# Places and load times of the contexts of a single-head attention, order of early loads, and who makes the first normalized chunks, in a four-layer transformer kernel

## The reference, cut to what matters

```python
# L0: keys and values from the normalized, modulated context
xkv = _ada_ln(x_kv, t_vec, Wss_kv, bss_kv)      # (x-mean)/sqrt(var+eps) * (1+scale) + shift
kv  = (xkv @ Wkv + bkv).reshape(B, Lkv, 2, nh, dh)
attn = softmax(einsum('bqhd,bkhd->bhqk', q, k) / sqrt(dh));  x = x + (attn @ v) @ Wp + bp
# L1: one head; the raw context is the prototype bank
nx = _layer_norm(x, ln_gamma, ln_beta);  q = nx @ Wq
k = prototype_bank @ Wk;  v = prototype_bank @ Wv
weights = softmax(einsum('bth,bph->btp', q, k) * H ** -0.5)
evidence = einsum('btp,bph->bth', weights, v)   # then a router, three experts and a gate
```

## Time and profile before

| | us |
|---|---|
| median of 3 runs (lowest, highest) | 958.58 (958.03, 962.11) |
| the profiled execution | 953.42 |
| its span, first to last instruction | 951.6 |
| TensorE busy in it | 839.7 (88%) |
| VectorE busy | 607.5 (64%) |
| ScalarE busy | 500.2 (53%) |
| GpSimd busy | 366.8 (39%) |
| chain of work that ended last: TensorE, VectorE, GpSimd, DMA | 61%, 16%, 6%, 3% |

### The profile page before, as it was taken

One profiled execution on the slowest core, in us unless ns is written; L12 is line 12 of the kernel. 1 busy time (PEld: TensorE's weight loads), 2 busy tenths in 40 slices (PEclk: granted clock), 3 DMA queues, 4 the chain that ended last, 5 costly groups with the idle time before them and its releaser, 6 DMA issues.

```text
span 951.6 us, 22830 instructions
## 1 busy us (share of the span) xinstructions
PE 839.7 (88%) x9532; PEld 543.2 (57%) x9532; DVE 607.5 (64%) x1274; ACT 500.2 (53%) x753; POOL 366.8 (39%) x482
## 2 busy tenths in 40 slices
PE   6689999998997897877999999888786799999986
PEld 4256677765655344534777776544452466666653
DVE  6877787776231663736777777535374677777825
ACT  7367777775232205234777776522413467767541
POOL 8666666630000034165666662010313333333000
PEclk9799999999899998878999999999788799999999
DMA  9954444357145106253444433010417244443100
GB/s 263 242 142 131 132 131 132 99 174 229 66 141 164 53 1 175 65 146 92 130 131 124 134 93 93 2 66 11 132 46 179 74 131 131 134 138 107 49 2 10
DMA packets 76838, 106.89 MB, mean 112 GB/s; under 512 B 9370, under 2 KB 70426, under 8 KB 76480
## 3 DMA queue, kind: packets, MB, share of 16 engines
q1 hardware_dynamic: 76016, 104.02, 39.7%
q10 hardware_dynamic: 720, 1.41, 0.5%
HBM read 41.56 MB, written 0.23 MB: 44 GB/s over the span
## 4 chain that ended last, share of the span: by engine, by line
PE 61%; DVE 16%; issue 8%; POOL 6%; ACT 4%; DMA 3%; SPq 1%; POOLq 0%; DVEq 0%; ACTq 0%
PE ring_ps L528 12%; PE oacc_ps L554 11%; PE score_ps L542 10%; PE ring_ps L512 6%; PE ring_ps L505 5%; DVE max_sb L657 4%; PE ring_ps L1163 3%; DVE tok L945 3%; PE ring_ps L497 2%; PE oacc_ps L321 2%; POOL hat_sb L723 2%; ACT prob_sb L631 1%; PE ring_ps L518 1%; DMA prob_sb<-ctx_T 1%; POOL kstack L1483 1%
## 5 line engine op out<-in xcount | busy, mean ns | idle before, releaser
L657 DVE TENSOR_REDUCE max_sb<-ring_ps 128x1 f32<-128x500 f32 x576 | 366.6, 674 | 134.6 <-PE ring_ps L528 132.5
L631 ACT ACTIVATE prob_sb<-score_ps 125x896 f32<-125x896 f32 x288 | 255.5, 919 | 86.8 <-PE score_ps L542 86.3
L528 PE MATMUL ring_ps<-kstack,qstack 128*128 128x500 bf16 x576 | 197.9, 388 | 28.0 <-DVE max_sb L657 9.3
L732 POOL TENSOR_TENSOR key_sb<-key_sb,part_sb 128x500 f32<-128x500 f32 x72 | 81.9, 1137 | 217.9 <-ACT key_sb L613 217.6
L542 PEld LDWEIGHTS score_ps<-qstack,kstack 128*128 128x128 bf16 (+1 forms) x2304 | 137.2, 102 | 49.2 <-issue 11.4
L542 PE MATMUL score_ps<-qstack,kstack 128*128 128x112 bf16 (+1 forms) x2304 | 158.2, 215 | 6.8 <-ACT prob_sb L631 5.0
L554 PE MATMUL oacc_ps<-prob_sb,val_sb 125*32 125x168 f32 (+1 forms) x3456 | 139.5, 294 | 1.7 <-ACT prob_sb L631 1.7
L554 PEld LDWEIGHTS oacc_ps<-prob_sb,val_sb 125*32 125x32 f32 x3456 | 97.5, 109 | 48.8 <-issue 20.6
L528 PEld LDWEIGHTS ring_ps<-kstack,qstack 128*128 128x128 bf16 x576 | 50.8, 98 | 95.9 <-issue 51.2
L723 POOL TENSOR_SCALAR hat_sb<-nat_sb,norm_now 125x128 f32<-125x128 f32 x192 | 87.2, 470 | 1.7
L1207 POOL TENSOR_TENSOR tok_rstd<-tok_var,minus_half 112x4 f32<-112x4 f32 x8 | 8.2, 1020 | 200.8 <-DVE tok_var L1221 200.7
(11 more groups left out here) (217 smaller groups left out, 989.7 us busy)
## 6 DMA issues: line engine op xcount, KB each, us to landing
kstack<-part_sb SPq DMA_DIRECT2D x432, 125.0 KB, 2.4
nat_sb<-ctx_nat SPq DMA_DIRECT2D x22, 672.0 KB
qstack<-qpart_sb SPq DMA_DIRECT2D x30, 224.0 KB, 3.7
nat_sb<-ctx_T SPq DMA_DIRECT2D x8, 750.0 KB, 5.2
w_sb<-ctx_nat SPq DMA_DIRECT2D x5, 672.0 KB
w_sb<-weights SPq DMA_DIRECT2D x1, 3268.5 KB, 13.1
prob_sb<-ctx_T SPq DMA_DIRECT2D x4, 750.0 KB, 7.8
tok<-ctx_nat SPq DMA_DIRECT2D x3, 672.0 KB
```

The costliest lines, as they stand in the source:

```text
L528: last = pe.matmul(ps[:, 0:KB], queries(p, n, D), kstack[:, u, p, j * KB:(j + 1) * KB], start=True, stop=True)
L631: ins = act.activation(dst, score_ps[0:CK, c % 2, :, 0:HALF], ACT.Exp)
L657: ins = dve.tensor_reduce(max_sb[:, p, j:j + 1], ring_ps[:, self.bank[name], 0:KB], AX.X, ALU.max)
L732: ins = pool.tensor_tensor(rest, rest, part_sb[:, 0, cols], ALU.subtract)
```

## The change

- In Evidence every context has a place of its own for the time it is needed, and each pair a semaphore. Transposed contexts 2 to 5 lie in key stack 0, natural 3 and 4 in `prob_flat`, natural 5 in key stack 0 again; `evi.sync` issues them in a new order, with a wait for the last scores (S11) of context 6.
- GpSimd clears key stack 0 after U2 and writes its two rows of ones; SP waits for that (`keys_restored`) before L2's context stacks.
- SP loads contexts 5 and 6 for the statistics behind the key stacks of context 0, and then the modulation weights, which ScalarE no longer issues.
- In L0's context 0 VectorE makes chunks 4 to 11 of `hat_sb`, after its modulation and ahead of q; GpSimd makes chunks 0 to 3 and for the rest waits (`hats_helped`) and writes a small cell.

```diff
@@ -305,6 +305,8 @@
         minus_half_keys = sb("minus_half_keys", [CK, NC])
         eps_keys = sb("eps_keys", [CK, 2, NC])
         minus_one_keys = sb("minus_one_keys", [CK, NC])
+        hats_seen = sb("hats_seen", [1, NJ])
+        hats_helped = sem("first_normalized_chunks_on_vector")
         consts_ready = sem("constants_ready")
         ev_t = T(6)
         logit = (q_t, k_t, o_t)
@@ -719,7 +721,10 @@
                             pool.wait_ge(self.nat_loaded[u], NAT_DMAS * (half + 1))
                             if nxt:
                                 pool.wait_ge(*self.after("pe", f"T{NJ - 1}", n - 1))
-                        for c in range(j * CJ, (j + 1) * CJ):
+                        if self.modulated and n == 0 and j:
+                            pool.wait_ge(hats_helped, j)
+                            ins = pool.memset(hats_seen[:, j:j + 1], 0.0)
+                        for c in range(j * CJ, (j + 1) * CJ) if not (self.modulated and n == 0 and j) else ():
                             ins = pool.tensor_scalar(hat_sb[:, c, :], nat_sb[0:CK, u, c, :], norm_now[:, 1, c:c + 1],
                                                     norm_now[:, 0, c:c + 1], ALU.add, ALU.mult)
                     else:
@@ -974,6 +979,10 @@
 
 
 
+        def key_stack(u):
+
+            return kstack[:, u, :, :].rearrange("p a k -> p (a k)").bitcast(F32)
+
         class Evidence:
 
 
@@ -987,16 +996,23 @@
                     *[f"PT{k}.{i}" for i in range(3)], *([f"E{k + 1}"] if k < 3 else []))]])
                 self.dve = Ticks(sem("ev_dve_done"), ["max0", "rec0", *[n for k in K for n in (
                     *([f"max{k + 1}"] if k < 3 else []), f"scale{k}", *([f"rec{k + 1}"] if k < 3 else []), f"out{k}")]])
-                self.loaded = [sem(f"ev_contextT_loaded{u}") for u in range(2)]
-                self.nat_loaded = [sem(f"ev_context_loaded{i}") for i in range(3)]
-                self.context = [tok[:, 7:11, :].rearrange("p a k -> p (a k)")[:, 0:NC * D]
-                                .rearrange("p (c k) -> p c k", k=D) if i == 2 else nat_sb[:, i, :, :] for i in range(3)]
+                self.loaded = [sem(f"ev_contextT_loaded{k}") for k in K]
+                self.nat_loaded = [sem(f"ev_context_loaded{k}") for k in K]
                 self.probs = key_sb[:, :]
                 self.scaled = T(6)[:, 0:D]
 
             def context_T(self, n):
 
-                return (ctxT_sb[:, :], part_flat[:, 0:S], prob_flat[:, 0:S], prob_flat[:, S:2 * S])[n % 4]
+                stack = key_stack(0)
+                return (ctxT_sb[:, :], part_flat[:, 0:S], *(stack[:, i * S:(i + 1) * S] for i in range(4)),
+                        ctxT_sb[:, :], part_flat[:, 0:S])[n]
+
+            def context(self, n):
+
+                size = NC * D
+                rows = (None, None, tok[:, 7:11, :].rearrange("p a k -> p (a k)")[:, 0:size], prob_flat[:, 0:size],
+                        prob_flat[:, size:2 * size], key_stack(0)[:, 0:size])
+                return nat_sb[:, n % 2, :, :] if n in (0, 1, 6, 7) else rows[n].rearrange("p (c k) -> p c k", k=D)
 
             def scores(self):
                 return score_ps[:, :, :, :].rearrange("p a b c -> p (a b) c")[:, 0:NJ, 0:KB]
@@ -1005,7 +1021,7 @@
                 P, A, V = self.pe, self.act, self.dve
 
                 def scores(k):
-                    pe.wait_ge(self.loaded[k % 2], 32 * (k // 2 + 1))
+                    pe.wait_ge(self.loaded[k], 32)
                     for j in range(NJ):
                         for t in range(2):
                             n = 2 * k + t
@@ -1040,15 +1056,13 @@
                     else:
                         keep_busy(pe, 4, score_ps[:, 0, 0, :])
                     pe.wait_ge(A.sem, A.after(f"PT{k}.2"))
-                    for t in range(2):
-                        n = 2 * k + t
-                        pe.wait_ge(self.nat_loaded[n % 3], NAT_DMAS * (n // 3 + 1))
+                    pe.wait_ge(self.nat_loaded[k], 2 * NAT_DMAS)
                     if k:
                         pe.wait_ge(V.sem, V.after(f"out{k - 1}"))
                     for c in range(NC):
                         for t in range(2):
                             last = pe.matmul(oacc_ps[64 * t:64 * t + 64, 0:D], hat_sb[:, c, 64 * t:64 * t + 64],
-                                             self.context[(2 * k + t) % 3][0:CK, c, :], start=(c == 0),
+                                             self.context(2 * k + t)[0:CK, c, :], start=(c == 0),
                                              stop=(c == NC - 1), skip_group_check=True)
                     P.done(last, f"U{k}")
                 keep_busy(pe, 3, ring_ps[:, 0, :])
@@ -1103,10 +1117,10 @@
                 P = self.pe
 
                 def turned(n):
-                    sp.dma_start(self.context_T(n), ctx_T[n]).then_inc(self.loaded[n // 2 % 2], 16)
+                    sp.dma_start(self.context_T(n), ctx_T[n]).then_inc(self.loaded[n // 2], 16)
 
                 def natural(n):
-                    load_context(sp, self.context[n % 3], n, self.nat_loaded[n % 3])
+                    load_context(sp, self.context(n), n, self.nat_loaded[n // 2])
 
                 natural(2)
                 sp.wait_ge(*a0.after("pool", f"hat{NJ - 1}", B - 1))
@@ -1118,17 +1132,19 @@
                     sp.wait_ge(a0.stacked[1][j], REPLICA * (B // 2))
                 sp.wait_ge(*a0.after("pool", f"k2.{NJ - 1}", B - 1))
                 turned(1)
+                sp.wait_ge(*a0.after("pe", f"S{NC - 1}", B - 2))
+                for n in range(2, 6):
+                    turned(n)
                 sp.wait_ge(*a0.after("pe", f"PV{NPV - 1}", B - 1))
-                turned(2)
-                turned(3)
-                for k in range(2):
-                    sp.wait_ge(P.sem, P.after(f"S{k}"))
-                    turned(2 * k + 4)
-                    turned(2 * k + 5)
-                    sp.wait_ge(P.sem, P.after(f"U{k}"))
-                    for n in ((3, 4), (5, 6))[k]:
-                        natural(n)
-                sp.wait_ge(P.sem, P.after("U2"))
+                natural(3)
+                natural(4)
+                sp.wait_ge(P.sem, P.after("S0"))
+                turned(6)
+                turned(7)
+                sp.wait_ge(P.sem, P.after("S1"))
+                natural(5)
+                sp.wait_ge(P.sem, P.after("U0"))
+                natural(6)
                 natural(7)
 
 
@@ -1397,13 +1413,10 @@
         a0, a2, a3 = att0, att_ctx["L2"], att_ctx["L3"]
         own2, own3 = att_own["L2"], att_own["L3"]
         buffers_ready = sem("buffers_ready")
-        def key_stack(u):
-
-            return kstack[:, u, :, :].rearrange("p a k -> p (a k)").bitcast(F32)
-
         queries_cleared = sem("query_buffers_cleared")
         values_cleared = sem("value_buffers_cleared")
         keys_cleared = sem("key_stacks_prepared")
+        keys_restored = sem("key_stack_restored")
         stats_loaded = {n: sem(f"statistics_context_loaded{n}") for n in range(2, B)}
         stats_done = sem("statistics_done")
         stats_kept = sem("statistics_kept")
@@ -1435,11 +1448,15 @@
             sp.wait_ge(loaded_early, 32)
             a0.load_nat(sp, 1, 1)
             sp.wait_ge(loaded_w0, 16)
-            for n in range(2, 7):
+            for n in range(2, STATS_FIRST):
                 load_context(sp, stats_buffer(n), n, stats_loaded[n])
             stack_queries(sp, queries_ready(d0), a0.qstacked, (0, 1))
             sp.wait_ge(keys_cleared, 1)
             a0.sync_batch(sp, None, (0, 0, 0), lambda: stack_queries(sp, queries_ready(d0), a0.qstacked, (2,)))
+            for n in range(STATS_FIRST, 7):
+                load_context(sp, stats_buffer(n), n, stats_loaded[n])
+            w0, w1 = W_AT["L2_W_mod"][0], W_AT["L1_Wq"][0]
+            sp.dma_start(w_sb[:, w0:w1], weights[:, w0:w1]).then_inc(loaded_wm, 16)
             sp.wait_ge(stats_done, STATS_AT[2] + 1)
             load_context(sp, stats_buffer(7), 7, stats_loaded[7])
             sp.wait_ge(keys_cleared, 2)
@@ -1454,6 +1471,7 @@
 
             sp.dma_start(w_sb[:, w1:w1 + L3_COLS], weights[:, W_L3:W_L3 + L3_COLS]).then_inc(loaded_w3, 16)
             own2.sync_shifts(sp)
+            sp.wait_ge(keys_restored, 2)
             a2.sync_batch(sp, None, (0, 0, 0))
             stack_queries(sp, queries_ready(d_mid["L2"]), a2.qstacked)
             a2.sync_later(sp)
@@ -1489,6 +1507,10 @@
             a0.later("pool", pool)
             pool.memset(own_val[:, :], 1.0).then_inc(buffers_ready, 1)
             d1.ln_pool(pool, "ln")
+            pool.wait_ge(evi.pe.sem, evi.pe.after("U2"))
+            pool.memset(kstack[:, 0, :, :].bitcast(F32), 0.0).then_inc(keys_restored, 1)
+            pool.wait_ge(keys_restored, 1)
+            pool.memset(key_stack(0)[SHIFT_ROW:SHIFT_ROW + 2, :], TWO_ONES).then_inc(keys_restored, 1)
             own2.gpsimd(pool, lambda eng: eng.wait_ge(*last_output(evi)), lambda eng: None)
             d2.ln_pool(pool, "own")
```

(9 more changed lines are left out.)

## The result

| us | before | after |
|---|---|---|
| median (lowest, highest) | 958.62 (958.03, 962.11), 4 runs | 946.38 (944.99, 947.32), 4 runs |
| the profiled execution, its span | 953.42, 951.6 | 944.99, 942.9 |
| ratio after / before, 95% interval | | 0.986 (0.9829 to 0.989) |

Forecast were 950.1 us and a range of 947.3 to 953.8. Between the two profiled executions the spans differ by 8.7, nearly the forecast. Both facts have to be explained, and the second is luck in part.

A forecast was written before the change was run, and what follows sets the result against it. TensorE starves at the start (key stack queued behind early loads, VectorE second latest) and in single-head attention (late context loads). Evidence 6.4 plus start 2.1 is 8.5 us, from 958.6 to 950.1; range 947.3 to 953.8.

The forecast's parts named there:

- the 5.2 us between it and the median: Whole kernel: the median's 5.2 us above the profiled execution was taken as carried over unchanged.
- the 6.4 us for Evidence: Single-head attention: no wait on a load remains, so U3 starts at 296.5 instead of 302.9, 6.4 us earlier.
- the 2.1 for the start: Start: first maximum 2.2 us earlier, less 0.1 for VectorE's chunks; 2.1 us, 0.5 to 2.6.
- S3's start, 2.8: Single-head attention: pair 3's scores start right behind UT1, not at 290.60; 2.8 us.
- S3 at the upper clock, 1.23: Single-head attention: pair 3's twelve score products take 2.74 us instead of 3.97; 1.23 us.
- U3's wait, 2.3: Single-head attention: pair 3's product with the contexts no longer waits for context 7's load; 2.3 us.
- S2 to S3 7.8 us apart: Single-head attention, a sign of success: scores of pairs 2 and 3 follow each other 7.8 us apart.
- The early issue: Evidence supply: transposed contexts 2 to 5, issued after context 6's S11, end near 245.5, far ahead of S1 at 272.2.
- I had 36.5 for it: Start: first maximum at 36.5, when VectorE's statistics end, instead of 38.66; 2.2 us gained.
- The exclusive lock: Start, late-q rival: VectorE's and GpSimd's chunks alternate on shared ports; start brings 0.7 us, time 951.6; chance 0.14.
- cost 0, from above 3 us: Context 1's key stacks: late loads of 3.9 MB end by 54 in an empty queue; cost 0, at most 3 us.
- the collision as a rival of 0.08: Context 1: late loads still in flight, its first M0.0 waits 2 to 4 us; 952 to 955; chance 0.08.

The follow-up runs named there:

- r2_evidence: Kernel before plus only the diff's Evidence places, semaphores, load order and restored key stack; 949.94 us, ratio 0.9896.
- r3_start: Kernel before plus only the start's part: late loads of contexts 5, 6 and modulation weights, and chunks on VectorE; 955.99 us, ratio 0.9964.
- r6_chunks: Kernel before plus only VectorE's chunks, without late loads or the Evidence part; 957.63 us, ratio 0.999.
- r5_defer: Kernel before plus only the late loads, without VectorE's chunks or the Evidence part; 957.73 us, ratio 0.9983.
- r1_before: Kernel before, unedited, timed and traced a second time; 958.65 us, ratio 0.9988.
- r10_swap: Kernel before, places and semaphores kept; SP issues transposed contexts 6 and 7 right behind S1, ahead of the natural ones; 957.16 us, ratio 0.9985.
- r4_after: The changed kernel, unedited, timed and traced again; 945.83 us, ratio 0.9855.
- r7_fill: Changed kernel plus eight products without use ahead of context 0's MT, to keep the clock up; 947.96 us, ratio 0.9873.
- r9_noearly: Changed kernel, but transposed contexts 2 to 5 go to their own places only behind context 7's last attention product; 946.5 us, ratio 0.9873.
- r11_stats: Changed kernel, only statistics 1 to 3 ahead of the first maximum; contexts 4; 5, 6; weights, 7 behind stacks of contexts 0, 1, 2; 941.84 us, ratio 0.9824.
- r8_late: Changed kernel with the late loads, all but context 5, put behind context 1's key stacks; 943.7 us, ratio 0.9841.
- r12_late_nochunks: Changed kernel with late loads except context 5 behind context 1's key stacks, and without VectorE's eight chunks; 946.41 us, ratio 0.9871.

## Why the prediction was wrong, point by point

**The base: the step that failed.** I priced every wait from one execution and then wrote that the 5.2 us between it and the median are carried over. They are not: for the most part they sit in the very waits that the change removes. The terms mis-sized by it are the 6.4 us for Evidence, which measured 9.5 by time (r2_evidence), and the 2.1 for the start, which measured 3.4 (r3_start). Ordered, S1 to U3 takes 30.73, 32.02, 32.72, 33.44 and 34.86 us in the traces of before, r3_start, r6_chunks, r5_defer and r1_before, and 24.28 or 24.29 in each of the eight traces of kernels with own places. At the middle one the stage is worth 32.7 - 24.3 = 8.4 us in the traces, not 6.4. Context 1's MT stands at 85.0, 86.0, 86.2, 87.7 and 88.4 in the five traces with the loads in the old order (before, r6_chunks, r1_before, r2_evidence, r10_swap) and at 83.7 to 84.8 in the five with the whole start part (after, r3_start, r4_after, r7_fill, r9_noearly): 86.2 - 84.0 = 2.2 us at the middle. Together 10.6 of the 12.2 us measured. Of the other 1.6, 1.2 can be the stretch behind L0: from the last MT to S0 the traces of the changed kernel are 1.2 us shorter than those of the kernel before, in each pairing of two with two (below). That leaves 0.4.

**Evidence, term by term.**
- S3's start, 2.8: the mechanism is right, the size is of the luckiest trace. The idle time was 2.63, 3.50, 3.96, 4.01 and 5.23 us in five traces, 4.0 in the middle.
- S3 at the upper clock, 1.23: right in direction; the cold products took 3.97 to 5.27 us, so the term is 1.2 to 2.5, but not in step with the wait ahead of it (4.03 us behind an idle time of 3.96, 4.43 behind 3.50).
- U3's wait, 2.3: right, 2.2 to 2.6 in the five.
- S2 to S3 7.8 us apart, S3's products 2.74, no DMA in the waits: all as said. The early issue, counted as part of the supply, isn't needed (r9_noearly).
- GpSimd's clears hold nobody up, and the two rows take 5.09 us, as put.

**Start: the first maximum better, the cost behind it missed.** I had 36.5 for it and it came at 35.41: q earlier by 0.56 (TensorE's fillers ahead of it took 3.23 us, not 3.62) and its split shorter by 0.4. The eight chunks took 0.27 us each, one behind the other without a pause, estimated at 0.3. Of GpSimd's own four the last two ran beside them and took 0.50 and 0.53 us, where one beside an idle VectorE took 0.44 in the trace of before; the first two took 0.90 or 0.91 and 0.84 in both kernels, beside VectorE's modulation of the tokens. The exclusive lock of the Trainium skill (SBUF — State Buffer, SBUF: two separate sides) would have had the chunks of the two engines alternate and left 0.7 us of the start; 0.7 is what the profiled pair shows at the end of L0, yet for another reason, and the rows here decide against that reading: less than 0.1 us was lost for each chunk.

A second step failed, without making the miss: the late loads at "cost 0, from above 3 us", with the collision as a rival of 0.08. Its sum stopped at the 3.9 MB, in flight until 54. It left out what comes behind them in the same queue: by the time the last stack of context 1's first column group is issued, its own earlier stacks of 0.125 MB each, issued from 49.2, stand behind those 3.9 MB too. Six of them are 0.75 MB or 3 us at 242 GB/s, and 54 becomes 57; r7_fill, where nothing else holds the product, shows the stack landed at 60.6, so even this count is short. The price of the queue alone is 1.4 and 2.5 us (r9_noearly, r7_fill, from context 0's MT to context 1's), partly within the 2 to 4 that I gave the rival, as a wait of 3.03 in r5_defer is. In the changed kernel itself the row shows a wait of only 0.47, since the value products ran slowly ahead of it, a cost of 1.7 alone that no term of the sum had; the two together took 2.0 of the 3.0 gained. The collision happened, and the total was too small all the same, since the base erred the other way by more.

**What I did not expect in an untouched stretch.** The eight products of the layer norm behind L0 (L1200 before, L1216 after) take 2.03 us before and 1.46 after, with 0.80 and 0.90 for the clock from 245 to 262 us; from the last MT of L0 to S0 it is 1.2 of the 8.7 us between the spans. 8.7 is thus 0.7 start, 1.2 behind L0, 6.4 Evidence and 0.4 in smaller shifts. Its agreement with 8.5 is luck: of the start's 2.1 only 0.7 was left, and 1.2 came from a stretch that I had not counted. The eight products are short in three traces, after, r4_after (1.17) and r11_stats (1.32); the other eleven have 2.03 to 2.05, among them r7_fill, r8_late, r9_noearly and r12_late_nochunks, all close to the changed kernel. No part of the diff goes with it, and what sets it is open.

## What to carry to other kernels

A wait that a late load ends is a draw from a range (2.63 to 5.23 us here), and one profile shows one draw: where the profiled execution stands under the median, look for the difference first in the waits that the change removes, and profile the old kernel a second time. A load moved out of the way of one consumer lands in front of the next: count until the last byte of that consumer's own transfers, small ones that queue behind it included. Where two causes hold the same instruction, taking away one shows nothing: look for a trace of each alone. If swapping two issues only trades waits, try more places.

## What the runs showed of the hardware that I had not expected

- In the split of q VectorE's product on 128 x 448 takes 0.75 or 0.76 us and the cast behind it 0.51 to 0.54 while GpSimd makes chunks, 0.62 or 0.63 and 0.39 or 0.40 while it is idle. It isn't always VectorE that pays: its modulation at 15.48 and 16.14 takes 0.62 beside GpSimd's first two chunks, and there the chunks take 0.90 and 0.84 instead of the 0.44 of one beside an idle VectorE. A 125 x 128 tensor_scalar with two vectors took 0.27 on VectorE beside GpSimd.
- GpSimd's memset of two rows of 6000 takes as long (5.09 us) as that of 128 rows (5.10).
- The same 24 value products after context 0's MT took 2.88 or 2.89 us in seven traces and 4.2 to 4.6 in the seven others, in kernels with and without each part of the change; what decides it is open.
